# A routed-experts and attention layer on one core: half of the first normalisation on GpSimd, and seven pairs of tiles turned by DMA transposes

## What is computed

```python
def reference(x, Wq, bq, Wkv, bkv, Wo, router_w, router_b, w1, b1, w2, b2):
    xn = layernorm(x)                      # over the 256 numbers of a row, eps 1e-5
    s = attention(xn, Wq, bq, Wkv, bkv, Wo)
    logits = xn @ router_w + router_b      # 8 experts, the top two are kept
    gating = softmax(where(top2(logits), logits, -1e30))
    h = relu(einsum("td,edh->eth", xn, w1) + b1)      # hidden size 1024
    y = einsum("eth,ehd->etd", h, w2) + b2
    g = silu(einsum("etd,te->td", y, gating))
    return x + s * g
```

## Time and profile before

| | |
|---|---|
| median of 3 runs | 1088.56 us (1087.25 to 1088.9) |
| the profiled execution | 1086.89 us |
| its span, first to last instruction | 1085.0 us |
| TensorE busy | 995.2 us, 92% of the span |
| VectorE busy | 859.1 us, 79% |
| ScalarE busy | 644.6 us, 59% |
| GpSimd busy | 324.9 us, 30% |
| granted TensorE clock | 0.999 of full speed |

### The profile page before, as it was taken

How to read it: one execution, slowest core, us unless ns; L and a number is a source line. 1 busy time by engine, 2 the same in 40 slices (tenths; PEclk the granted TensorE clock), 3 DMA queues, 4 the chain that set the end, 5 groups by cost and what they waited for, 6 DMA issues and landing times.

```text
span 1085.0 us, 25159 instructions
## 1 busy us (share of the span) xinstructions
PE 995.2 (92%) x8734; PEld 783.7 (72%) x8734; DVE 859.1 (79%) x1543; ACT 644.6 (59%) x1360; POOL 324.9 (30%) x339
## 2 busy tenths in 40 slices
PE   1647999999999999998889889999999999999997
PEld 1536888888888898965656667767677677777776
DVE  6885777666766555569999999998999999999971
ACT  3812333233333333348888888878888888888860
POOL 0005999899994200020011102121112111112111
PEclk9999999999999999999999999999999999999999
DMA  8548776766665312137897888998999879898992
GB/s 281 178 192 182 154 186 172 173 175 178 178 171 157 89 50 55 37 102 147 165 162 141 158 159 177 164 149 153 171 185 178 148 147 170 160 173 160 175 183 90
DMA packets 402810, 168.80 MB, mean 156 GB/s; under 512 B 345562, under 2 KB 393252, under 8 KB 402052
## 3 DMA queue, kind: packets, MB, share of 16 engines
q1 hardware_dynamic: 345632, 127.04, 56.1%
q10 hardware_dynamic: 50580, 22.45, 8.6%
q0 software_dynamic: 6480, 17.70, 6.6%
HBM read 51.66 MB, written 30.67 MB: 76 GB/s over the span
## 4 chain that ended last, share of the span: by engine, by line
PE 35%; DVE 13%; DMA 3%; ACT 3%; issue 2%; SPq 0%; ACTq 0%; DVEq 0%
PE b_psS L1144 10%; PE b_psO L1167 10%; PE b_psJ L1183 5%; PE b_psJ L1101 4%; DVE b_ph L1383 4%; DVE b_nmax L1347 4%; DMA b_pT<-b_ph 3%; PE b_psS L1194 2%; PE b_psS L1101 1%; PE b_psO L1169 1%; DVE b_outs L1389 1%; ACT b_pr L1252 1%; ACT b_ph L1282 1%; DVE b_psJ L1356 1%; PE b_psS L1147 1%
## 5 line engine op out<-in xcount | busy, mean ns | idle before, releaser
L847 PE MATMUL psU<-bxT,w_p 128*128 128x256 f16 (+1 forms) x1920 | 287.9, 263 | 13.3 <-DVE w_p L273 10.4
L922 ACT ACTIVATE h<-psU,bias 128x256 f32<-128x256 f32 (+1 forms) x320 | 124.7, 447 | 284.9 <-PE psU L847 192.8
L856 PE MATMUL psY<-w_p,hp 128*128 x1704 | 272.4, 273 | 1.8 <-DVE hp L944 1.3
L1144 PE MATMUL b_psS<-b_kp,b_Q 128*128 128x512 f16 (+3 forms) x1152 | 218.4, 326 | 0.1
L847 PEld LDWEIGHTS psU<-bxT,w_p 128*128 x1920 | 189.1, 98 | 33.8 <-issue 15.1
L1252 ACT ACTIVATE b_pr<-b_psS,b_nmax 128x1024 f32<-128x1024 f32 (+7 forms) x256 | 186.7, 734 | 42.4 <-DVE b_nmax L1347 22.8
L1167 PE MATMUL b_psO<-b_pT,b_vp 128*128 128x256 f16 x1536 | 188.6, 272 | 18.1 <-issue 8.4
L1383 DVE SCALAR_TENSOR_TENSOR b_ph<-b_pr,b_rrec,b_ph 128x1024 f16<-128x1024 f32 (+7 forms) x256 | 199.1, 809 | 0.0
L1282 ACT ACTIVATE b_ph<-b_pr,b_rrec 128x1024 f16<-128x1024 f32 (+7 forms) x256 | 187.0, 768 | 15.9 <-DVE b_rrec L1376 15.6
L942 DVE CAST hp<-h 128x512 f16<-128x512 f32 (+1 forms) x160 | 88.5, 553 | 134.0 <-ACT h L922 127.1
L1347 DVE TENSOR_REDUCE b_nmax<-b_psS 128x1 f32<-128x1024 f32 (+7 forms) x256 | 182.7, 745 | 9.2 <-PE b_psS L1147 7.3
(11 more groups left out here) (181 smaller groups left out, 1029.4 us busy)
## 6 DMA issues: line engine op xcount, KB each, us to landing
wstage<-in_L_ffn_w SPq DMA_DIRECT2D x48, 256.0 KB
expert_rows<-rowx SPq DMA_DIRECT2D x67, 128.0 KB
expert_outputs<-y ACTq DMA_DIRECT2D x31, 256.0 KB
a_x_all<-in_L_attn_x SPq DMA_DIRECT2D x8, 512.0 KB, 9.8
a_w_raw<-in_L_ffn_w SPq DMA_DIRECT2D x4, 1024.0 KB, 6.5
xn_split<-a_xp SPq DMA_DIRECT2D x4, 1024.0 KB, 4.9
xn_turned<-a_xT SPq DMA_DIRECT2D x3, 1024.0 KB, 12.8
b_x_row<-in_L_attn_x SPq DMA_DIRECT2D x24, 128.0 KB, 2.6
```

Of the source, the lines that this page charges most:

```text
L847: mm = eng.matmul(psU[w % U][:, g % 2, 0:tiles * P].rearrange("p (t r) -> p t r", t=tiles), weight(n, a * W1 + c * H + g * P, P), bxT[n % ...
L856: mm = eng.matmul(psY[n % 2][:, t, :], hp[n % 2][:, a, g, t * P:(t + 1) * P], weight(n, 2 * W1 + (2 * g + b) * D, D), start=(g == 0 and k ...
L922: a = eng.activation(h32[w % 4][:, g, 0:rows], psU[w % U][:, g, 0:rows], ACT.Relu, bias=bias[:, ds(e * HT + 2 * q + g, 1)], scale=1.0 / WS)
L1144: mm = eng.matmul(dst, Q[n % 3][:, a, u * P:(u + 1) * P], kb[:, c, lo:lo + w], start=(kk == 0), stop=(kk == 2 and not last))
```

## The change

In the first stage, pairs 0 to 7 are normalised by GpSimd, with the same instruction that VectorE used; VectorE goes on to the remaining statistics and then makes the low halves of pairs 0 to 3, and from pair 8 on it alternates `normal(p)` with `low(p - 4)`. The even pairs 0 to 12 (`BY_DMA`) are turned by DMA transposes from `xp` in SBUF to `turned(p)` in SBUF, issued by SyncE when the pair's low half is there; at most four are under way. They stand in SyncE's queue ahead of the stores of `xn_split`. TensorE turns the other nine (`BY_PE`), with a new order of turns and logits; eight of these are copied out by ScalarE and one, pair 14, by VectorE. The order on ScalarE is written out by a table (`behind`), with the second square root behind `high(5)`. TensorE's wait for the router's low half (`s_rl`) moves to the start of its queue, and the store of `xn_turned` waits for one more pair, now that pairs may be finished by either way.

```diff
@@ -344,7 +344,9 @@
     bq, bkv, rw, rb, w1, b1, w2, cst, pe = (v[k] for k in ("bq", "bkv", "rw", "rb", "w1", "b1", "w2", "cst", "pe"))
     COLS, PER, HALF = 2 * NT, 8, NT // 2
     CHUNKS, TWOS, LOADS = COLS // PER, NT // 2, 8
-    OUT_DVE = (TWOS - 3, TWOS - 1)
+    BY_DMA = tuple(range(0, TWOS - 2, 2))
+    BY_PE = tuple(p for p in range(TWOS) if p not in BY_DMA)
+    OUT_DVE = (TWOS - 2,)
     PARTS = NT * E // P
     ROWS = E * HT + HEADS + 2
     area = Arena(v["nc"], v["raw_end"])
@@ -403,6 +405,8 @@
     psR = psX[:, 0:(NT + 1) * E]
     s_x = [sem(f"x_loaded{i}") for i in range(LOADS)]
     s_w = [sem(f"w_in{i}") for i in range(4)]
+    s_dt = [sem(f"turned_by_dma{i}") for i in range(4)]
+    s_xp = sem("xn_by_pool")
     (s_c, s_ct, s_br, s_pe, s_z, s_one, s_bn, s_var, s_sd, s_rs, s_xn, s_xh, s_ld, s_t, s_ea, s_ed, s_cc, s_tab) = map(sem, (
         "tables_in", "prefix_table_in", "biases_in", "positions_in", "zeroed", "ones", "stats", "variance", "std", "rstd",
         "xn", "xn_hi", "xn_lo", "turned", "out_by_act", "out_by_dve", "casts", "tables_cast"))
@@ -420,22 +424,25 @@
 
     def out_done(eng, p):
 
-        if p in OUT_DVE:
+        if p in BY_DMA:
+            eng.wait_ge(s_dt[p // 2 % 4], 16 * (p // 8 + 1))
+        elif p in OUT_DVE:
             eng.wait_ge(s_ed, before(p, OUT_DVE))
         else:
-            eng.wait_ge(s_ea, p + 1 - before(p, OUT_DVE))
+            eng.wait_ge(s_ea, before(p, BY_PE) - before(p, OUT_DVE))
 
     def low_done(eng, p):
 
         eng.wait_ge(s_ld, p + 1)
 
     def on_tensor(eng):
-        def turn(p):
-
+        def turn(e):
+
+            p = BY_PE[e]
             low_done(eng, p)
-            if p >= 4:
-                out_done(eng, p - 4)
-            bank = turn_bank[p % 4].bitcast(F16)
+            if e >= 4:
+                out_done(eng, BY_PE[e - 4])
+            bank = turn_bank[e % 4].bitcast(F16)
             for t in range(2):
                 for h in range(2):
                     for c in range(DC):
@@ -446,8 +453,6 @@
         def logits(p):
 
             out_done(eng, p)
-            if p == 0:
-                eng.wait_ge(s_rl, 1)
             for i in range(2):
                 t, k = 2 * p + i, 0
                 for a, b in PASSES:
@@ -481,13 +486,17 @@
                 mm.then_inc(s_sp, 1)
 
         eng.wait_ge(s_cc, 4)
-        for p in range(TWOS):
-            turn(p)
-            if p == 3:
+        eng.wait_ge(s_rl, 1)
+        for e in range(len(BY_PE)):
+            turn(e)
+            if e == 1:
                 eng.wait_ge(s_br, 80)
                 eng.transpose(psJ[:, 0:ROWS], brow[:, :], c_sb[0:ROWS, 0:ROWS]).then_inc(s_b, 1)
-            if p >= 2:
-                logits(p - 2)
+            if 1 <= e <= 7:
+                logits(BY_PE[e - 1])
+            if e >= 2 and e - 2 < len(BY_DMA) - 1:
+                logits(BY_DMA[e - 2])
+        logits(BY_DMA[-1])
         logits(TWOS - 2)
         logits(TWOS - 1)
         eng.wait_ge(s_bz, 3)
@@ -497,13 +506,21 @@
 
     def on_scalar(eng):
         def high(p):
-            eng.wait_ge(s_xn, p + 1)
+            if p < TWOS // 2:
+                eng.wait_ge(s_xp, p + 1)
+            else:
+                eng.wait_ge(s_xn, p - TWOS // 2 + 1)
             sl = slice(2 * p, 2 * p + 2)
             eng.activation(xp[:, sl, 0, :], x_all[:, sl, :], ACT.Copy).then_inc(s_xh, 1)
 
         def out(p):
-            eng.wait_ge(s_t, p + 1)
-            eng.activation(turned(p).rearrange("p t h n -> p (t h n)"), turn_bank[p % 4].bitcast(F16), ACT.Copy).then_inc(s_ea, 1)
+            eng.wait_ge(s_t, BY_PE.index(p) + 1)
+            eng.activation(turned(p).rearrange("p t h n -> p (t h n)"), turn_bank[BY_PE.index(p) % 4].bitcast(F16), ACT.Copy).then_inc(s_ea, 1)
+
+        def root(k):
+            sl = slice(k * HALF, (k + 1) * HALF)
+            eng.wait_ge(s_var, k + 1)
+            eng.activation(rs[:, 0, sl], mv[:, sl, 1], ACT.Sqrt, bias=eps[:, :]).then_inc(s_sd, 1)
 
         def weights(q):
             eng.wait_ge(s_w[q // 4], 16)
@@ -525,23 +542,22 @@
             eng.activation(dst, src, ACT.Copy).then_inc(s_cc, 1)
         eng.wait_ge(s_br, 80)
         eng.activation(rw_p[:, 0], rw_s[:, :, :], ACT.Copy, scale=WS).then_inc(s_rh, 1)
-        for k in range(2):
-            sl = slice(k * HALF, (k + 1) * HALF)
-            for p in range(k * TWOS // 2, (k + 1) * TWOS // 2):
-                if p == k * TWOS // 2:
-                    eng.wait_ge(s_var, k + 1)
-                    eng.activation(rs[:, 0, sl], mv[:, sl, 1], ACT.Sqrt, bias=eps[:, :]).then_inc(s_sd, 1)
-                high(p)
-                if p >= 2 and p - 2 not in OUT_DVE:
-                    out(p - 2)
-                if p == 7:
-                    eng.wait_ge(s_b, 1)
-                    eng.activation(bias[:, 0:E * HT], psJ[:, 0:E * HT], ACT.Copy).then_inc(s_bz, 1)
-                    eng.activation(bias[:, E * HT:ROWS - 1], psJ[:, E * HT:ROWS - 1], ACT.Copy, scale=SC).then_inc(s_bz, 1)
-                    eng.activation(bias[:, ROWS - 1:], psJ[:, ROWS - 1:ROWS], ACT.Copy).then_inc(s_bz, 1)
-        for p in (TWOS - 2, TWOS - 1):
-            if p not in OUT_DVE:
-                out(p)
+        behind = {7: 1, 8: 3, 9: 5, 11: 7, 13: 9, 15: 11}
+        root(0)
+        for p in range(6):
+            high(p)
+        root(1)
+        for p in range(6, TWOS):
+            high(p)
+            if p in behind:
+                out(behind[p])
+            if p == 9:
+                eng.wait_ge(s_b, 1)
+                eng.activation(bias[:, 0:E * HT], psJ[:, 0:E * HT], ACT.Copy).then_inc(s_bz, 1)
+                eng.activation(bias[:, E * HT:ROWS - 1], psJ[:, E * HT:ROWS - 1], ACT.Copy, scale=SC).then_inc(s_bz, 1)
+                eng.activation(bias[:, ROWS - 1:], psJ[:, ROWS - 1:ROWS], ACT.Copy).then_inc(s_bz, 1)
+        out(TWOS - 3)
+        out(TWOS - 1)
         eng.wait_ge(s_ct, 16)
         for dst, src in ((tri16[:, :, :], c_sb[:, C_TRI:].rearrange("p (h t) -> p h t", t=TRI)),
                          (lane16[:, :, :], lanes.unsqueeze(2).to_broadcast([P, P, PER])),
@@ -606,15 +622,8 @@
             eng.tensor_tensor(xp[:, sl, 1, :], x_all[:, sl, :], xp[:, sl, 0, :], ALU.subtract).then_inc(s_ld, 1)
 
         def out(p):
-            eng.wait_ge(s_t, p + 1)
-            eng.tensor_copy(turned(p).rearrange("p t h n -> p (t h n)"), turn_bank[p % 4].bitcast(F16)).then_inc(s_ed, 1)
-
-        def after(p):
-
-            if 0 <= p - 1 < TWOS:
-                low(p - 1)
-            if p - 3 in OUT_DVE:
-                out(p - 3)
+            eng.wait_ge(s_t, BY_PE.index(p) + 1)
+            eng.tensor_copy(turned(p).rearrange("p t h n -> p (t h n)"), turn_bank[BY_PE.index(p) % 4].bitcast(F16)).then_inc(s_ed, 1)
 
         def wide_e(a):
             return a.unsqueeze(2).to_broadcast([P, NT, E])
@@ -719,25 +728,20 @@
         variance(HALF, slice(0, HALF))
         stats(4)
         rstd(1, slice(0, HALF))
-        for p in range(4):
-            normal(p)
-            after(p)
         for g in (5, 6, 7):
             stats(g)
-            if g == 5:
-                eng.wait_ge(s_rh, 1)
-                eng.scalar_tensor_tensor(rw_p[:, 1], rw_s[:, :, :], WS, rw_p[:, 0], ALU.mult, ALU.subtract).then_inc(s_rl, 1)
-            normal(g - 1)
-            after(g - 1)
         variance(NT, slice(HALF, NT))
-        normal(7)
-        after(7)
+        eng.wait_ge(s_rh, 1)
+        eng.scalar_tensor_tensor(rw_p[:, 1], rw_s[:, :, :], WS, rw_p[:, 0], ALU.mult, ALU.subtract).then_inc(s_rl, 1)
+        for p in range(4):
+            low(p)
         rstd(2, slice(HALF, NT))
         for p in range(8, TWOS):
             normal(p)
-            after(p)
-        for p in range(TWOS, TWOS + 3):
-            after(p)
+            low(p - 4)
+        for p in range(TWOS - 4, TWOS):
+            low(p)
+        out(TWOS - 2)
         choose(0)
         choose(1)
         eng.wait_ge(s_tot, 1)
@@ -758,6 +762,11 @@
     def on_gpsimd(eng):
         eng.memset(eps[:, :], EPS).then_inc(s_z, 1)
         eng.memset(one16[:, :], 1.0).then_inc(s_one, 1)
+        eng.wait_ge(s_rs, 1)
+        for p in range(TWOS // 2):
+            for t in (2 * p, 2 * p + 1):
+                a = eng.tensor_scalar(x_all[:, t, :], x_all[:, t, :], mv[:, t, 0:1], rs[:, 0, t:t + 1], ALU.subtract, ALU.mult)
+            a.then_inc(s_xp, 1)
         eng.wait_ge(xs_, 64)
         eng.wait_ge(v["who_"], 1)
         for n in range(4):
@@ -770,6 +779,12 @@
         eng.dma_start(w_raw[0][:, 0:4, :].rearrange("p (c g) n -> p c (g n)", c=DC), w1[0].rearrange("(c p) n -> p c n", p=P)).then_inc(s_w[0], 16)
         eng.wait_ge(s_x[7], 16)
         eng.dma_start(w_raw[0][:, 4:8, :].rearrange("p q (g d) -> p (q g) d", d=D), w2[0].rearrange("(g p) d -> p g d", p=P)).then_inc(s_w[1], 16)
+        for d, p in enumerate(BY_DMA):
+            low_done(eng, p)
+            if d >= 4:
+                eng.wait_ge(s_dt[d % 4], 16 * (d // 4))
```

(3 more changed lines are left out.)

## The result

The changed kernel takes 1092.92 us in the median of 20 runs (1088.79 to 1097.74), the kernel before 1087.74 us (20 runs, 1085.79 to 1095.13): a ratio of 1.0048 [1.0036, 1.0061]. It is 5.2 us slower, where 4.4 us less was forecast. The profiled execution took 1092.29 us with a span of 1090.5.

A forecast was written before the change was run, and what follows sets the result against it. VectorE was taken to bound the first stage and routing, TensorE the experts. Choose moving from 49.02 to 44.3 us won 4.7, less 0.3 for ScalarE's exponential: 4.4 us, from 1088.56 to 1084.2 us; range 1081.8 to 1088.3.

The forecast's parts named there:

- GpSimd's price: First stage: one normalised tile on GpSimd estimated at 0.48 us, the middle of half of L258 and the whole.
- The upper end, 1.45 us for two tiles: First stage: high end kept for GpSimd normalising two tiles, 1.6 us with gaps; the low end was 0.64.
- P: First stage: GpSimd's time to normalise a pair of two tiles, taken as 1.0 us.
- R: Start of VectorE's second half: at least 19.5 + 6P; 25.9 us, or 27.1 with contention, against 34.47 before.
- rival 1: GpSimd bounds the first half: P = 1.6, R = 30.2, 1087.3 us; break-even at P = 2.1; chance 0.18.
- R + 17.2: End of the first stage: choose starts 17.2 us after the second half starts, at 44.3 us.
- Of the 8.7 + 3.7 us: First half: time VectorE is freed or moved forward; 4.7 us won at choose, the rest used up later.
- Contention: First stage: VectorE's four low halves beside GpSimd's last pairs pay 0.29 us each, 1.2 us; statistics pay 0.
- L = 4.5: DMA transposes: estimated landing time in us; at this value the seven transposes cost nothing.
- Rival 3: SyncE's queue of transposes drains more slowly than low halves come; at worst 1102 us; chance 0.09.
- They start from that gather: Stages behind the routing: tied to no time of day, they start from GpSimd's gather for the experts.
- rival 4: Behind the first stage: the gain is waited for at a load of weights or a store; 1088.5 us; chance 0.08.

The follow-up runs named there:

- m2_forms: Kernel before, with GpSimd instructions on scratch tiles added in front, one pair of operations after another; 1088.05 us, run once.
- f1_add: Changed kernel with the mean stored negated and normalisation by add and multiply on GpSimd and VectorE; ratio to before 1.0014, repeated 1.0004.
- e4_root_early: Changed kernel with the second square root behind ScalarE's second cast instead of its sixth; 1091.74 us, run once.
- e2_dma_only: Changed kernel without GpSimd's half: DMA transposes kept, VectorE normalises all pairs; ratio to before 1.0037, repeated 1.0055.
- g3: g1 with TensorE turning all tiles, so without the DMA transposes; ratio to before 0.9964.
- g1: f1_add with a lead: GpSimd splits the first two pieces of expert weights ahead of the gather that waits; 1081.29 us, ratio to before 0.9951.
- b1: Kernel before with the four stores of xn_split held back to the low half of pair 13; ratio to before 1.0009.
- d1: Kernel before with ten more small VectorE additions chained ahead of the routing, so choose starts 4.4 us later; ratio to before 1.0054.
- g5: Changed kernel with the same two-piece lead in GpSimd's weight splitting as g1; 1089.50 us, ratio to before 1.0031.
- m1: Kernel before, with GpSimd scratch-tile operations added in front, in the changed kernel's own form and some near it; 1087.38 us, run once.
- f2_add_pe: f1_add with TensorE turning all tiles and no DMA transposes; ratio to before 1.0020.

## Why the prediction was wrong

- **GpSimd's price: the step that failed.** "Half of L258" to "the whole of it", 0.48 us, came from a row with another pair of operations. The text said that no row had this form, and then took L258 as "the same operation"; both are TENSOR_SCALAR, but L258 multiplies twice, and the change subtracts and multiplies. Measured: 1.30 us a tile with gaps (1.21 median). m2_forms takes the width, the scalars' place and the operations apart: L258's own form takes 0.65 us there as it does in the kernel, the change's 1.22, and add with multiply, alike in width and scalars, 0.555. The upper end, 1.45 us for two tiles, was too low as well: it took the two-input L1472 for a ceiling. With P = 2.6 the text's own formula gives R = 19.5 + 15.6 = 35.1; measured 35.75. P was beyond the break-even of 2.1 that rival 1 named: the mechanism was rival 1's, its size was outside what it allowed.
- **The sum behind it held for a cheap tile, and by luck for the dear one.** In f1_add `choose` is at R + 17.3, forecast R + 17.2; the forecast has 44.3, f1_add 45.5. In the changed kernel R + 17.2 gives 52.95, measured 53.6, but e4_root_early has R = 30.24 and the same end. The forecast let GpSimd hold the second half only through `high(5)` and the root; that ScalarE's last cast of the first half waits for GpSimd's last pair, and that 15.4 us of work follow it, was no term of the sum. At 1.30 us a tile the two ways happen to end together.
- **A sentence without a working.** "Of the 8.7 + 3.7 us" has none. The gain of 4.7 us follows from R alone: 34.47 - 27.1 = 7.4 us earlier, less a tail of 17.2 us where that of before is 14.55 (34.47 to 49.02).
- **Contention: most of it falls elsewhere than charged.** The forecast let VectorE's four low halves pay 1.2 us. In f1_add two of the four took 1.05 and 0.96 us instead of 0.68, 0.65 us more together, and two tiles of GpSimd beside them took 1.50 us, where the 13 ahead of them took 0.56:

```profile
L768 POOL TENSOR_SCALAR a_x_all<-a_x_all,a_mv,a_rs x13: 556/561/602, 17.2 to 23.7; 128x256 f32<-128x256 f32 x13
...
L768 POOL TENSOR_SCALAR a_x_all<-a_x_all,a_mv,a_rs x2: 1503/1504/1504, 24.2 to 25.7; 128x256 f32<-128x256 f32 x2
...
23.75 3.14 DVE L622 TENSOR_TENSOR a_xp<-a_x_all,a_xp 128x512 f16<-128x512 f32 x4
```

In the changed kernel all low halves keep 0.67 to 0.69 us, and two GpSimd tiles that run beside them take 1.88 and 1.81 us against 1.21. The 12 statistics (4.01 us, so 1.34 for four) are not longer than in the earlier trace rows. VectorE's small steps are, which had no term: in the changed kernel the six of rstd take 2.1 us where the earlier trace rows have 1.2 (L611 0.50 us where the same step takes 0.17), and in f1_add the variance step takes 2.5 us (21.18 to 23.66) instead of 1.0. That is most of why f1_add's R is 28.25 and not 27.1.
(The Trainium skill, page "SBUF — State Buffer", section "Who interferes with whom", has a two-input VectorE instruction contend with a GpSimd one that reads SBUF, and issue order decide which of them blocks. The trace agrees: where the low halves keep their 0.68 us it is GpSimd's tile that grows, by 0.66 and 0.59 us in the changed kernel. Page "GPSIMD Engine Reference", section "4.1 Engine selection", calls a one-input operation on GpSimd roughly line-rate; in m2_forms one and the same shape goes from 0.40 to 1.22 us by the pair of operations, and VectorE does it in about 0.33, half of 1.26 - 0.60 in the earlier trace rows. The measurement decides.)
- **The DMA transposes: right.** No wait of TensorE for one; 2.7 to 4.3 us from issue to landing, inside L = 4.5 (in e2_dma_only one took 6.8). Rival 3 didn't come. What they bring, though, is under 1 us (g3 against g1). The stores behind them cost nothing that b1 can tell.
- **"They start from that gather": half right.** The experts do start with it, and a late start is paid in full (d1, g5). An early start isn't got in full, as f1 shows; the lead gives it back, so it is GpSimd's splitting of the weights, which the forecast never priced, that has too little slack. TensorE's 393.57 of 400 us was read as "nothing else binds there"; it only says that nothing else bound at the old start. This is near rival 4, "waited for at a load of weights or a store", which had 0.08. It would have taken the gain even of a cheap GpSimd form, so the forecast time was out of reach for a second reason.
- **The profiled pair misleads about where.** At the experts' last row the changed kernel is only 0.6 us behind (472.0, 471.4); the 5 us come after. Its attention stage has the same instructions, though. From the last row to the end of the span it takes 618.5 us, before 613.6; other kernels made from the one before, with nothing changed behind the routing, take 614.3 (d1), 616.5 (m1), 618.1 (b1) and 618.2 (m2). The two shortest, before and d1, are the only profiles of all with a granted clock of 1.00 from 490 to 580 us; the changed kernel has 0.94, and so has f1, here second:

```profile
490.00:580.00 90.00, 78.96 (x598) 52.89 (x597) 86.84 (x155) 76.86 (x158) 9.40 (x10) 1.00 0.84 158
```

```profile
490.00:580.00 90.00, 79.03 (x570) 52.46 (x571) 82.16 (x147) 73.22 (x150) 8.51 (x9) 0.94 0.86 152
```

So one and the same code moves an execution by some 4 us, and the expert stage's length (377.8 to 388.2 us in the table) varies too; only medians of many runs carry a verdict of this size.

## What to carry over

Price a moved instruction by a row with the same operations in it, not only the same name, engine and shape; where none is there, measure the form alone first, and try the algebraic twin (add the negated mean). A stage that seems bound by one engine may have a second one just behind it: before you shorten what lies ahead of it, look for the producer with no rest (here GpSimd, 36.9 of 40 us) and give it a lead, because only the two edits together gave a gain, 4.9 us. The best kernel of this study is g1_add_lead, 1081.3 us.

## What the runs showed of the hardware

- GpSimd's tensor_scalar at 128x256 f32: 0.40 us (mult, mult, constants), 0.547 (mult, mult from SBUF), 0.555 (add, mult or mult, add), 0.92 (one operation), 1.22 (subtract, mult).
- Beside it VectorE's statistics kept their duration, and two-input low halves kept 0.68 us or took up to 1.05; the GpSimd tile beside them grew from 1.21 to 1.88 us (subtract, mult) and from 0.56 to 1.50 us (add, mult). VectorE's steps on 128x16 took up to 0.55 us instead of 0.17.
- DMA transposes of 128x1024 f16 from SBUF to SBUF landed in 2.7 us, at worst 4.3, issued at 1.23 to 1.34 us each in the changed kernel; in e2_dma_only one took 6.8 us.
- TensorE's granted clock stayed at 1.00 across a wait of 1.17 us and was at 0.66 and 0.79 over the ten us from 270 to 280 with the waits of 3.29 and 6.33 us (f1_add, f2_add_pe), at 1.00 in the ten before.
